# Query and key units taken in turns, and weighted values ahead of the side work, in the attention pairs that stand alone

## The reference

```
x  = L0_attn_x                                  # (8, 512, 256)
xn = layernorm(x)
x  = x + attn0(xn) + moe0(xn)                   # 16 heads of 16; latent q/k, causal softmax; 8 experts, top 4
xn = layernorm(x)
x  = x + attn_sparse(xn) + attn_moe1(xn)        # causal sparsemax attention, 16 heads
                                                # attn_moe1: rope, grouped attention (16 heads, 4 of keys),
                                                # residual, rmsnorm, 8 experts, top 2
```

## Time and profile before

| | |
|---|---|
| median of 3 runs | 3105.05 us (3104.85 to 3107.97) |
| the profiled execution, its own time | 3129.51 us |
| span of its trace | 3127.6 us |
| mean granted TensorE clock | 0.956 |
| busy: PE, DVE, ACT, POOL | 2809.4, 2133.4, 1615.2, 1506.6 us |

### The profile page before, as it was taken

The page is one execution under the profiler, slowest core; times in us unless marked ns, Lnnn a source line. Parts: engine busy times, 40 slices in busy tenths (PEclk is TensorE's granted clock), DMA queues, the critical chain, the costliest instruction groups (busy, mean ns, idle before and its releaser), DMA issues. The chain is left out here.

```text
span 3127.6 us, 61182 instructions
## 1 busy us (share of the span) xinstructions
PE 2809.4 (90%) x20990; PEld 2275.6 (73%) x20990; DVE 2133.4 (68%) x6013; ACT 1615.2 (52%) x3388; POOL 1506.6 (48%) x2213
## 2 busy tenths in 40 slices
PE   5877799999999999978998898998799999999996
PEld 3555478888899889846666666666588888888864
DVE  6878678788788788767777877766644444454565
ACT  3544344444454445545655555655455555555553
POOL 4768743443343354385556666322233333332487
PEclk8878799999999999989999999999899999999998
DMA  3555578788888888422333344210466666665355
GB/s 83 197 208 202 196 262 311 278 286 316 284 290 307 294 286 308 178 40 55 97 99 104 105 107 109 93 69 22 164 213 210 228 213 212 204 241 203 124 97 126
DMA packets 212008, 580.13 MB, mean 185 GB/s; under 512 B 24617, under 2 KB 146417, under 8 KB 167409
## 3 DMA queue, kind: packets, MB, share of 16 engines
q1 hardware_dynamic: 172528, 523.82, 47.7%
q0 software_dynamic: 36864, 51.14, 8.1%
q10 hardware_dynamic: 2304, 1.21, 0.1%
HBM read 450.14 MB, written 125.96 MB: 184 GB/s over the span
## 5 line engine op out<-in xcount | busy, mean ns | idle before, releaser
L1139 POOL TENSOR_TENSOR al<-t,ah 128x512 fp32r<-128x512 f32 x220 | 283.4, 1288 | 875.1 <-ACT ah L1375 875.1
L481 PE MATMUL bank<-xh,gu 128*128 128x256 f32 x3520 | 672.3, 291 | 33.6 <-DVE gc L1654 25.8
L481 PEld LDWEIGHTS bank<-xh,gu 128*128 128x128 f32 x3520 | 512.6, 190 | 57.7 <-issue 55.0
L524 PE MATMUL bank<-masks_bf,ident_bf 128*128 128x128 bf16 x1896 | 432.9, 252 | 133.9 <-DVE st L1840 41.0
L1840 DVE TENSOR_REDUCE st<-bank 128x1 f32<-128x512 f32 (+3 forms) x1024 | 422.1, 481 | 166.1 <-PE bank L542 158.6
L1472 ACT ACTIVATE pt<-bank 128x512 f32<-128x512 f32 (+1 forms) x1152 | 512.0, 540 | 30.2 <-PE bank L545 21.9
L524 PEld LDWEIGHTS bank<-masks_bf,ident_bf 128*128 128x128 bf16 x1896 | 170.3, 99 | 353.6 <-DVE st L1840 95.3
L1480 ACT ACTIVATE oT<-bank 128x512 f32<-128x512 f32 x192 | 114.6, 597 | 602.5 <-PE bank L621 576.5
L542 PE MATMUL bank<-ksT,qsT 128*128 128x512 f32 (+3 forms) x1536 | 410.3, 369 | 5.7 <-DVE top L1838 3.1
L545 PE MATMUL bank<-qaT,ksT 128*128 128x512 f32 (+3 forms) x1536 | 399.6, 372 | 0.0
L481 PE MATMUL bank<-xl,gu 128*128 128x256 f32 x1760 | 351.5, 281 | 0.0
(11 more groups left out here) (250 smaller groups left out, 5216.2 us busy)
## 6 DMA issues: line engine op xcount, KB each, us to landing
gu<-wu_scratch SPq DMA_DIRECT2D x110, 1032.0 KB, 5.2
gu<-wu_scratch SPq DMA_DIRECT2D x110, 1024.0 KB, 7.4
dn<-wd_scratch SPq DMA_DIRECT2D x110, 1024.0 KB, 6.7
xs<-xs_scratch SPq DMA_DIRECT2D x110, 264.0 KB, 4.3
ys_scratch<-yb SPq DMA_DIRECT2D x110, 256.0 KB, 7.0
raw<-in_gu SPq DMA_DIRECT2D x16, 1024.0 KB
wu_scratch<-hi SPq DMA_DIRECT2D x16, 1024.0 KB
wu_scratch<-lo SPq DMA_DIRECT2D x16, 1024.0 KB
```

Of the source, the lines that this page charges most:

```text
L481: mm = pe.matmul(bank[:, TS * h:TS * (h + 1)], gu[:, col:col + P], x[s % 2][:, TS * k:TS * (k + 1)], start=(n == 0), stop=(n == len(terms) ...
L524: return pe.matmul(S.bank((which, G, u))[:, diag:diag + P * len(unit)], ident_bf[:, :], masks_bf[:, side, 0:len(unit), :].rearrange("p n k ...
L1139: pool.tensor_tensor(em["al"][s % 2][:, m, :], em["t"][g % 2][:, :], em["ah"][s % 2][:, m, :].bitcast(F32), ALU.subtract).then_inc(al_read ...
```

## The change

In `pair_alone` three orders change. PE makes two query units of pair G + 1 first and then a key unit of pair G and a query unit in turns: q0 q1 k0 q2 k1 q3 k2 q4 k3 q5 k4 k5 (the last pair and the general variant for rare inputs keep the old order). O of pair G − 1 moves from behind the query units to before the side work: behind Ta in mla and gqa, before Ta in spm. ACT's `take_o` moves in the same way. The condition under which masks are added last is rewritten so that the same units have it as before. DVE and POOL keep their programs.

```diff
@@ scores
-                    masks_last = which == "q" and len(S.banks) == len(units)
+                    masks_last = which == "q" and (G - 1 in plan or general)
@@ pair_alone, PE
-                    shifted(G)
+                    if is_at(n, "spm"):
+                        if G and G - 1 not in plan:
+                            outputs(G - 1)
+                        shifted(G)
+                    else:
+                        shifted(G)
+                        if G and G - 1 not in plan:
+                            outputs(G - 1)
...
-                    if G + 1 < steps:
+                    if G + 1 == steps or general:
+                        if G + 1 < steps:
+                            keys_in(G + 1)
+                            scores("q", G + 1, range(NU))
+                        pe.wait_ge(x_act, X.count[f"Ta{G}"])
+                        scores("k", G, range(NU))
+                    else:
                         keys_in(G + 1)
-                        scores("q", G + 1, range(NU))
-                    if G and G - 1 not in plan:
-                        outputs(G - 1)
-                    pe.wait_ge(x_act, X.count[f"Ta{G}"])
-                    scores("k", G, range(NU))
+                        scores("q", G + 1, range(2))
+                        pe.wait_ge(x_act, X.count[f"Ta{G}"])
+                        for u in range(NU):
+                            scores("k", G, [u])
+                            scores("q", G + 1, range(u + 2, min(u + 3, NU)))
@@ pair_alone, ACT
-                    take_qa(G)
+                    if is_at(n, "spm"):
+                        if G and G - 1 not in plan:
+                            take_o(G - 1)
+                        take_qa(G)
+                    else:
+                        take_qa(G)
+                        if G and G - 1 not in plan:
+                            take_o(G - 1)
...
-                    if G and G - 1 not in plan:
-                        take_o(G - 1)
```

## The result

The changed kernel takes **3208.21 us** (median of 4 runs, 3199.1 to 3210.93), the kernel before 3104.95 in the same series: a ratio of 1.0329, 95% interval 1.0308 to 1.035, or 103 us slower. 3174 had been forecast, with a range from 3108 to 3225 in all and 3135 to 3205 for the forecast's own case. The profiled execution of the changed kernel took 3205.72 us (span 3204.2, mean clock 0.943).

A forecast was written before the change was run, and what follows sets the result against it. The prediction took PE as the bound with some 10% of holes, DVE ending most of its waits. Batches 57, routing 15, first layer's last pairs 4, other stretches −3, end −4: +69 on the median gave 3174 us, range 3108 to 3225.

The forecast's parts named there:

- routing: Pairs before 406 us: +15 us (bounds 0 and 50), from even pairs; odd pairs, 0 to 3.5 us each, taken at 0.
- Shift at N + 0.73: DVE's shift would end 0.73 us after PE's transpose N of the former pair's output, instead of 1.0 us before it.
- banks at N + 2.8, 3.9 and 4.9: Position 3: two transposes would get banks at N + 2.8 and 4.0 us, weighted values theirs at N + 4.9.
- bare own-key pairs: Pairs with own keys and no side work would fall from about 8.45 to 7.16 us, −1.3.
- The first rival: Faster if N's bank is nowhere late: −45 us, 3060 us; decided at S = 0.45 us; chance 15%.
- S: DVE's work between shift and heads_out; from 0.45 us on values wait; larger in five of eight positions.
- Both rings bite: ACT's late exponents cost 3.5 us per odd routing pair and the clock falls at each new stall: +115, 3220 us; 13%.
- At the new stalls less work follows before the next one: Clock loss at new stalls in positions 5 and 7: 0.7 us each, against 1.07 us seen for values; bounds 0 and 2.
- N's bank: Bank of the former output's transpose, returned by heads_out; values with own keys would ask for it at N + 1.76 us.
- I add the difference to the median: The +69 us, summed on a profiled execution of 3129.51 us, were added to the 3105.05 us median.
- the coupling of the shared score ring in position 3: ACT's squares would delay k0's exponents, and through the shared banks k2, q4 and all behind them by 1.0 us.
- The two rules: Matmuls keep program order, otherwise the sum is 6 us less; ACT and DVE reading PSUM at once adds nothing.

The follow-up runs named there:

- e2: Changed kernel with all six query units ahead of the key units again, weighted values still ahead of the side work: 3140.69 us, ratio 1.0121.
- e6: Changed kernel with the key units two places further back (q0 q1 q2 q3 k0 q4 k1 q5 k2 to k5): 3149.33 us, ratio 1.0146.
- the second profile: The kernel before, unchanged, profiled once more: the profiled execution took 3102.41 us, against 3129.51 us in the first.
- e8: Changed kernel with GpSimd's root of the hidden mean moved behind the next key stack: 3210.97 us, ratio 1.0348.
- e3: Changed kernel with DVE's heads_out moved ahead of the rotation, hidden mean and rows, head squares and other later side work: 3197.69 us, ratio 1.0308.
- e4: The kernel before with DVE's heads_out moved ahead of the rotation, hidden mean and rows and other later side work: 3185.2 us, ratio 1.0267.
- e11: Changed kernel with ACT's split of the routing weights (odd pairs) moved from ahead of the exponents to behind them: 3195.21 us, ratio 1.0286.
- e10: Changed kernel with key units two places further back and the rotation moved behind heads_out on DVE: 3108.52 us, ratio 1.0017.
- e12: Kernel before, with e6's order in positions 0, 1 and 5 of grouped batches (pairs 72 to 121) and the p = 5 rotation behind heads_out: 3105.2 us.
- e9: The kernel before with the changed order in 18 pairs alone, the others keeping the old order: 3102.88 us, ratio 0.9998.

## Why the prediction was right, and where it was too small

**The sum was short by a third.** The measured 103 us lie inside the whole range, but 3208 is 3 us above the forecast's own range of 3135 to 3205, and nearer to the rival at 3220 than to 3174. By the stretches in the table, 12.4 us are missing in the six batches, 10.2 in routing and 12.2 in the two stretches beside the six batches.

**The place and the mechanism held.** Shift at N + 0.73, banks at N + 2.8, 3.9 and 4.9 in position 3, bare own-key pairs at 7.3 and 7.4 us (pairs 63 and 64; forecast 7.16, before 8.4 and 8.7), and batches of 93.0 us (forecast 90 to 94). The first rival, faster because DVE's lead is enough, needed S under 0.45 us; e2 and e6 show that each part of the lead that is lost costs. "Both rings bite" (3220 us) is close in time, and its two conditions hold in part: the odd routing pairs cost 12 us, not 35, and the clock falls behind the new stalls.

By position, in two batches, from N to N, less the same pairs in the first trace of before:

| position | forecast | pairs 105 to 112 | pairs 113 to 120 |
|---|---|---|---|
| 1 | +0.7 | −0.2 | −0.2 |
| 2 | −0.1 | −0.2 | 0.0 |
| 3 | +2.7 | +4.2 | +3.8 |
| 4 | −0.3 | −0.4 | −0.4 |
| 5 | +2.0 | +3.3 | +2.3 |
| 6 | +1.7 | +2.9 | +3.4 |
| 7 | +1.0 | +3.8 | +2.2 |
| 0 | +0.4 | +0.4 | 0.0 |
| sum | +8.1 | +13.8 | +11.1 |

The same differences against the second profile sum to +14.0 and +10.9.

**Mis-sized: the clock.** I took 1.4 us a batch, 0.7 for each of two stalls. Position 7 of the changed kernel shows more. PE waits for DVE's selection and `heads_out`, then works at the lower level:

```profile
2003.12 1.95 PE L621 MATMUL bank<-pt,V 128*17 128x512 f32 x16 [2.39 <-DVE both L1940]
...
2007.27 0.78 PE L545 MATMUL bank<-qaT,ksT 128*128 128x512 f32 x1
...
2010.69 0.47 PE L545 MATMUL bank<-qaT,ksT 128*128 128x512 f32 x1
```

The windows of the wait and of the work behind it:

```profile
1998.83:2002.99 4.16, 1.90 (x17) 1.67 (x16) 3.73 (x15) 1.30 (x4) 1.87 (x5) 1.00 0.04 13
2003.12:2009.80 6.68, 6.68 (x35) 4.25 (x36) 2.17 (x6) 3.46 (x7) 3.36 (x3) 0.53 0.45 94
```

The granted clock is 1.00 in the window that holds the wait and 0.53, near the lower of its two levels (1.2 GHz), for the 6.68 us after. A key unit takes 0.78 us there and 0.47 once the clock is back. From the first mask to N the units take 6.0 us instead of 4.2 and values 1.95 instead of 1.27: 2.5 us. In position 6 the units take 5.5 instead of 4.2: 1.3 us. In position 3 values and projection lose 1.07 + 0.57 = 1.6 us. Together 5.4 us a batch, four times what I took, if these positions stand for all six batches; PE's busy time gives 3 on the mean (below). The step that failed is "At the new stalls less work follows before the next one": what follows is a whole projection or a whole set of score units. Since the score units set when DVE can start its maxima, the slower clock would also sit on the path of the cycle; no run tests that by itself.

**Missed: who waits behind the waiting one.** I followed the late shift to N's bank and not to DVE's other products. The hidden mean goes to GpSimd, whose stack for position 6 stands behind two gathers and a scatter. PE waits for it in five of the six batches (13.7 us), and in two of them position 5 comes out over 3 us longer where 2.0 had been forecast. By e8 removing it alone wins nothing: position 5 gets no shorter. e3 and e4 show how large this side is.

**Mis-sized: routing.** Forecast +15 (0 to 50), measured +25.2. Against the first profile it would be 514.4 − 508.6 = +5.8. The sum was made on an execution that had by chance lost 19 us in this very stretch, so "I add the difference to the median" mixed two bases. e11 shows that the odd pairs, which I had taken at 0 (their bound was 35), cost 12.

**Too large:** the coupling of the shared score ring in position 3. I took 1.0 us; the masks wait 0.46 us for ACT there. Positions 1 and 0 were overstated by 0.9 and up to 0.4 us.

**The two rules.** Key and query units keep their written order in every timeline: one waiting query unit holds the keys behind it, and the wait for the maxima now ends at k1 (3.0 us in position 0), as forecast. Maxima and exponents now read PSUM at the same time, for 90.6 us in the six batches where they never did before; the mean of a maximum goes from 481 to 485 ns and that of an exponent from 549 to 526:

```profile
L1858 DVE TENSOR_REDUCE st<-bank 128x1 f32<-128x512 f32 (+3 forms) x384 | 165.0, 485 | 146.5 <-PE bank L542 146.3
...
L1485 ACT ACTIVATE pt<-bank 128x512 f32<-128x512 f32 (+1 forms) x288 | 145.6, 526 | 136.1 <-PE bank L545 132.0 <-PE bank L542 0.8
```

So adding nothing for it was right. The Trainium skill, "PSUM — Partial Sum Buffer", specifications, says that the two engines read different banks in parallel at full bandwidth; the trace agrees. The last row also shows the price on ACT: it idles 136.1 us ahead of exponents.

**What stays open.** In the six batches PE's listed waits rise by 41.6 us (46.3 in the second profile of before, 87.9 in the changed kernel), of 69.4. How the other 28 split between the clock and the interleaving itself: PE's busy time rises by 30.5 us over the second profile, and by 12.6 in e10, where the clock is 0.98 as before. About 18 us would then be the clock's, 3 a batch on the mean, against the 5.4 that I put together from single positions. Nor is it shown what the last 5 us of e10 are. They are not in the six batches, which are level with before (488.4 and 488.9 us; positions 2, 6 and 7 longer, 0, 1 and 5 shorter). Its profile is 4.6 us behind at pair 24, so routing is where to look.

## What to carry to other kernels

When two engines share a ring of banks, write down by how much the reader's last step leads the writer's next request, and what the reader does in that time. An interleaving that removes a wait of one engine can spend another's lead: here the filled wait was 0.9 us, in pairs with keys of their own, and with DVE's order unchanged each us of lead was worth 6.6 us a batch of eight pairs. Before moving a step, ask of each product of the delayed engine who waits for it; move the piece for which nobody does soon (here the rotation, 58 us), and only where the lead is gone: in e12 the same move in pairs 61 and 69, where DVE still led by 0.7 and 1.0 us, made the pairs behind them 2.2 and 2.8 us longer. And profile the kernel before twice when its profiled execution is not near the median.

## What the runs showed that I had not expected

A stall of 2.4 us on PE was followed by 6.7 us of work at a granted clock of 0.53, and the fall came after the stall, not in it (1.00 in the window that holds it). In e9 a longer wait, 4.61 us, shows part of the fall already inside it: 0.77 from 1383.0 to 1387.6 us, 0.50 behind it. Eighteen pairs made shorter, most of them by 0.5 to 1.4 us, changed the time by 0.02%: behind pairs 56 and 64 PE waits for rows that DVE makes, and the new order makes these rows later. Two executions of one kernel differed by 26.7 us of span (3127.6 and 3100.9), 19.4 us of it before pair 24, while the medians of its runs lay between 3102.9 and 3105.05 us.
